# A Mamba stage on one core: two sequences as one run of 18 rounds, the output product moved within the round, its squares summed first, and the projection blocks spread anew

## The chip, the cores and the metric

The kernel runs on one core of one Trainium2 chip. The metric is the device time of one execution of the whole program in microseconds (us): everything from the first load to the last store. Engines are named as in the profile: PE is TensorE (PEld its weight loads), DVE is VectorE, ACT is ScalarE, POOL is GpSimd, SP issues the DMAs.

## What is computed

The program is a small model of two layers: a Mamba-2 block, a gated MLP, a second gated MLP with weights from a 16-entry table, an attention of 16 heads, and a mixture of 8 experts. The change touches the Mamba block alone. It works on 2 sequences (batches) of 1024 tokens, 256 wide, in float32:

```
zxbcdt = x @ in_proj_w
z, xb, Bc, Cc, dt = split(zxbcdt)                  # 512, 128, 128, 512, 8 columns
xBC = silu(causal_depthwise_conv([xb, Bc, Cc]))    # 4 taps, 768 channels
dt = softplus(dt + dt_bias);  A = -exp(A_log)
# for each chunk of 128 tokens and each of 8 heads (head size 64, state size 64):
#   Y_diag = (C B^T * exp(seg), masked) @ (x dt)      inside the chunk
#   Y_off  = exp(cum) * C @ state                     from the chunks before
#   state  = decay * state + B^T @ (decayed x dt)     goes to the next chunk
y = Y_diag + Y_off + D * x
y = rmsnorm(y * silu(z)) @ out_proj_w
```

The state begins at zero for each of the two sequences, and the convolution sees zeros before the first token of each.

## The kernel before

**Tiling.** Tokens come in 16 tiles (chunks) of 128, 8 for each sequence, and in 4 groups of 512. A float32 product is made of three passes of split operands (high by high, high by low, low by high; `three_passes`, L53 to L55). For each group of 512 tokens the input projection gives ten blocks of 128 channels: six that go through the convolution (m = 0 to 5, "conv") and four of the gate z (m = 6 to 9, "z"). One conv block is six matmuls on PE, two evacuations on ACT (L1048, L1051), three taps and a small copy on DVE (L1127, L1132 or L1134), a tanh on ACT (L1100), and a last product on DVE that writes `xbc` (L1194, `conv_end`), one block later. One z block is six matmuls, a tanh on ACT (L1059) and one product on DVE (L1142).

**The chunk.** A chunk n is worked in three events, in three successive rounds. Event A, on PE: two transposes (L965), the broadcast of the cumulated decay `rows` (L972, which waits for `steps` of POOL, made anew each four chunks, L1245), the scores C B^T (L980, which wait until `mixed` of the chunk before is done, since they overwrite its bank), and the mask (L986, which waits for `row_exp`); on ACT the copy `xb_tok` (L1064), `row_exp` (L1069) and the eight exponentials `decay` (L1075). `A_end`, on DVE: `mixed` = decay times scores, eight instructions (L1149). Event B: the products y (L999 and L1005) and the new state's product (L1014) on PE; the state's update and `gated` (L1156 to L1170) on DVE; `gated_hi` and `squares` on ACT (L1082, L1083); `gated_lo` on POOL (L1267). Event C: the output product (12 matmuls, L53 to L55 with `out_hi`, `out_lo`) and behind it the sum of the squares (4 products with a vector of ones, 8 instructions in the trace, L1026), both into one bank; DVE makes `out_var` (L1174), POOL `out_root` (L1263), and in `C_end` DVE scales and adds (`u_tok`, L1178).

**What sets the order.** Each engine has its own instruction stream, written out by `sequence_steps` in one list that all engines follow; waits are semaphores. Round c holds, in this order: A(c); then the projection blocks of place 0; B(c-1) and C(c-2); place 1 (empty); A_end(c) and C_end(c-2); the blocks of place 2. `SPREAD` puts the ten blocks of the next group into four rounds: conv 0, 1 | conv 2, 3 | conv 4 ahead of B, conv 5 and z 6 behind | z 7 ahead of B, z 8 and 9 behind. The rounds run from 0 to 9 for each sequence: two more than there are chunks, so that B and C of the last ones are done. A loop of one turn (`Fori`) does the first sequence, and the code is written out once more for the second. All ten blocks of the very first group come ahead of the first round.

**Banks.** Projection blocks and C share two PSUM banks in turn (`with_banks`): a block waits until the user before last of its bank is finished with on ACT or DVE. B has bank 5, the scores have 2 and 3, rows and mask 0 and 1.

**Around it.** In the second sequence, rounds 5 and 6 also hold the splitting of MLP weights (`feed`: ACT L1088, POOL L1219 to L1228), and rounds 7 to 9 the norm of the first MLP group (stats L155 to L165, apply L202, turn L224, split L238). SP loads those weights when all projections and convolutions are done, and the inputs of the table stage when the whole Mamba stage is done.

Of the kernel before, what the change touches and what calls it, by code (L numbers as in the profile page):

```python
# [14 lines left out]
P = 128  # L15
# [684 lines left out]
def mamba_stage(nc, sems, mem, s, w, dma, u, ff, norm_next):  # L700
# [11 lines left out]
    def sb(what, shape, dt=F32):  # L712
# [5 lines left out]
             "xdt_decayed skip_ready y_ready y_taken state_ready state_done gated gated_hi squares gated_lo out_ready out_var "  # L718
# [32 lines left out]
    SPREAD = ((2, 2), (2, 2), (0, 2, 2), (0, 2, 2))  # L751

    QUARTERS = 4
    FEED_AT = {5: (0, 1), 6: (2, 3)}
    NORM_AT = {7: ("stats",), 8: ("apply", "turn"), 9: ("split",)}
    NORM_BANK = 2

    def sequence_steps(last):


        steps = []
        for c in range(CHUNKS + 2):
            group = c // TG + 1
            blocks = []
            if group <= (1 if last else GB):
                first = sum(len(x) for x in SPREAD[:c % TG])
                blocks = [(place, ("project", group, first + n)) for n, place in enumerate(SPREAD[c % TG])]
            parts = [[("A", c, None)] if c < CHUNKS else [],
                     ([("B", c - 1, None)] if 1 <= c <= CHUNKS else []) + ([("C", c - 2, None)] if c >= 2 else []),
                     ([("A_end", c, None)] if c < CHUNKS else []) + ([("C_end", c - 2, None)] if c >= 2 else [])]  # L770
            for place, part in enumerate(parts):
                steps += part + [e for at, e in blocks if at == place]
            if last:
                steps += [("feed", c, n) for n in FEED_AT.get(c, ())] + [("norm", c, n) for n in NORM_AT.get(c, ())]
        return steps

    first_steps = [("project", 0, m) for m in range(IP)]
    PER = dict(conv=GB * XBC_BLOCKS, z=GB * Z_BLOCKS, chunk=CHUNKS)
# [5 lines left out]
    def with_banks(events):  # L784


        ring = [e for e in events if e[0] in ("project", "C")]
        assert len(ring) % 2 == 0
        at = {e: n for n, e in enumerate(ring)}
        users = [("C", e[1], None) if e[0] == "C_end" else e for e in events]  # L790
        return [(e, s.psum[:, 6 + at[user] % 2, :], ring[at[user] - 2] if at[user] >= 2 else None) if user in at
                else (e, None, None) for e, user in zip(events, users)]

    def sequences(engine, step, start=None):

        for e in with_banks(first_steps):
            step(0, *e)
# [5 lines left out]
        if start:  # L803
            start(BATCH - 1)
        for e in with_banks(sequence_steps(True)):
            step(BATCH - 1, *e)

# [118 lines left out]
    def tensor(pe):  # L926
# [10 lines left out]
        def step(b, e, bank, old):  # L937
            kind, c, m = e
            n = CHUNKS * b + (c or 0)
            par = (c or 0) // TG % 2  # L940
            q = slice((c or 0) % TG * P, (c or 0) % TG * P + P)
            if kind in ("project", "C"):

                if old is None and c != 0:

                    pe.wait_ge(done["out_done"], CHUNKS * b)
                    pe.wait_ge(done["gate_done"], PER["z"] * b + Z_BLOCKS)
                elif old is not None and old[0] == "C":
                    pe.wait_ge(done["out_done"], CHUNKS * b + old[1] + 1)
                elif old is not None:  # L950
# [1908 lines left out]
```

## Time and profile before

| | us |
|---|---|
| median of 3 runs (lowest, highest) | 1872.57 (1870.99, 1872.8) |
| the profiled execution | 1873.78 |
| its span in the profile | 1872.0 |
| from the first projection block to the end of `mixed` of chunk 1 | 58.38 to 111.52 |
| from there to the end of `mixed` of the last chunk | 111.52 to 332.32 |
| from there to the first product of the MLP | 332.32 to about 349.7 |

The profile is one execution. Its page gives the busy time of each engine over the span; the stage of this case takes 58 to 350 us of 1872. A good mark for the rounds is the end of `mixed` (the eight DVE instructions of L1149): it comes once in each round, and the time from one to the next is called an interval here.

### The profile page before, as it was taken

The numbers are of one execution on the slowest core, as the hardware profiler recorded it, in microseconds if no ns is written. First come the engines' busy times: TensorE is split into PE (matmuls) and PEld (weight loads), VectorE is DVE, ScalarE is ACT, GpSimd is POOL, SyncE is SP. The second block draws the span as 40 slices with busy tenths as digits, with TensorE's granted clock in tenths as the row PEclk, the third lists the DMA queues.
The fourth block names the chain that finished last, engine by engine and source line by source line (L and its number), as shares of the span: only waits on it lengthen the run. The fifth ranks groups of instructions, "written<-read, shape, count | busy, mean of one in ns | idle before, by whom it ended". The sixth has DMA issues, their size and how long they took to land.

```text
span 1872.0 us, 31589 instructions
## 1 busy us (share of the span) xinstructions
PE 1623.4 (87%) x9546; PEld 1356.6 (72%) x9546; DVE 1246.1 (67%) x2797; ACT 972.2 (52%) x2046; POOL 656.7 (35%) x727
## 2 busy tenths in 40 slices
PE   3578778788899999999999997999999999858795
PEld 2345444677788878888888886788888888746584
DVE  6677474678965666666666675766666666758585
ACT  3355354355533375666666754656666666424242
POOL 5133336433433342223222312322233222355652
PEclk9789788899999999999999998999999999879897
DMA  3000001200010420000000000010000000231243
GB/s 108 1 1 1 1 1 46 63 12 14 5 21 1 107 70 17 8 22 22 22 0 22 6 18 23 1 46 2 22 22 22 0 22 6 84 125 57 95 135 128
DMA packets 78383, 64.53 MB, mean 34 GB/s; under 512 B 16656, under 2 KB 72704, under 8 KB 78288
## 3 DMA queue, kind: packets, MB, share of 16 engines
q1 hardware_dynamic: 74544, 53.08, 10.0%
q0 software_dynamic: 3744, 10.26, 1.5%
q8 instruction: 50, 0.82, 0.2%
q14 instruction: 45, 0.37, 0.1%
HBM read 44.89 MB, written 18.43 MB: 34 GB/s over the span
## 4 chain that ended last, share of the span: by engine, by line
PE 64%; DVE 17%; issue 6%; ACT 5%; DVEq 3%; POOL 3%; DMA 1%; POOLq 0%; ACTq 0%; SPq 0%
PE psum L53 10%; PE psum L55 10%; PE psum L54 10%; PE psum L1687 6%; PE psum L1700 3%; PE psum L1677 3%; PE psum L1679 3%; PE psum L1678 3%; PE psum L1701 3%; PE psum L1708 3%; DVE table_leaves L589 2%; DVE mamba_conv_sum L1127 2%; POOL moe_slots_x L2173 2%; DVE mamba_mixed L1149 2%; PE psum L999 1%
## 5 line engine op out<-in xcount | busy, mean ns | idle before, releaser
L1888 POOL TENSOR_SCALAR attn_probs<-attn_probs,attn_inverse 128x128 f32<-128x128 f32 (+7 forms) x256 | 192.3, 751 | 543.6 <-DVE attn_inverse L1839 543.6
L1756 ACT ACTIVATE attn_pt_hi<-psum 128x512 fp32r<-128x512 f32 (+3 forms) x384 | 185.4, 484 | 182.7 <-PE psum L1687 181.9
L1761 ACT ACTIVATE attn_probs<-attn_probs,attn_neg_max 128x128 f32<-128x128 f32 (+7 forms) x256 | 198.4, 775 | 134.0 <-DVE attn_neg_max L1811 131.5
L1807 DVE TENSOR_TENSOR attn_pt_lo<-psum,attn_pt_hi 128x512 fp32r<-128x512 f32 (+3 forms) x384 | 211.8, 553 | 43.1 <-ACT attn_pt_hi L1756 39.4
L1687 PE MATMUL psum<-ident,attn_probs 128*128 128x128 f32 x1152 | 194.0, 278 | 15.5 <-DVE x_tok L1847 11.9
L1811 DVE CUSTOM_DVE_ANT_0 attn_probs<-psum,attn_mask 128x128 f32<-128x128 f32 (+7 forms) x256 | 192.7, 753 | 20.1 <-PE psum L1679 10.6
L1700 PE MATMUL psum<-attn_pt_hi,attn_v_hi 128*128 128x512 f32 (+3 forms) x384 | 161.2, 420 | 21.7 <-DVE attn_pt_lo L1807 12.4
L1687 PEld LDWEIGHTS psum<-ident,attn_probs 128*128 128x128 f32 x1152 | 140.3, 142 | 40.3 <-issue 12.9
L417 POOL TENSOR_TENSOR gated_h_lo<-gated_hidden,gated_h_hi 128x512 fp32r<-128x512 f32 x56 | 79.6, 1421 | 161.0 <-ACT gated_h_hi L402 161.0
L1677 PE MATMUL psum<-attn_k_hi,attn_q_hi 128*128 128x512 f32 (+3 forms) x384 | 133.6, 348 | 2.6 <-DVE attn_neg_max L1811 2.4
L1701 PE MATMUL psum<-attn_pt_lo,attn_v_hi 128*128 128x512 f32 (+3 forms) x384 | 134.4, 350 | 0.0
L1679 PE MATMUL psum<-attn_k_hi,attn_q_lo 128*128 128x512 f32 (+3 forms) x384 | 133.5, 348 | 0.0
L1678 PE MATMUL psum<-attn_k_lo,attn_q_hi 128*128 128x512 f32 (+3 forms) x384 | 133.4, 347 | 0.0
L1708 PE MATMUL psum<-attn_pt_hi,attn_v_lo 128*128 128x512 f32 (+3 forms) x320 | 116.0, 362 | 0.0
L1881 POOL TENSOR_TENSOR attn_qkv_lo<-attn_qkv_raw,attn_qkv_hi 128x512 fp32r<-128x512 f32 x45 | 57.9, 1289 | 153.6 <-ACT attn_qkv_hi L1738 153.6
L53 PE MATMUL psum<-act_hi,attn_qkv_hi 128*128 128x512 f32 x256 | 105.5, 412 | 4.4 <-POOL attn_qkv_lo L1881 2.2
L55 PE MATMUL psum<-act_hi,attn_qkv_lo 128*128 128x512 f32 x256 | 102.5, 400 | 0.0
L54 PE MATMUL psum<-act_lo,attn_qkv_hi 128*128 128x512 f32 x256 | 102.3, 400 | 0.0
L1700 PEld LDWEIGHTS psum<-attn_pt_hi,attn_v_hi 128*128 128x128 f32 x384 | 74.1, 193 | 31.5 <-DVE attn_pt_lo L1807 16.8
L402 ACT ACTIVATE gated_h_hi<-gated_hidden 128x512 fp32r<-128x512 f32 x56 | 35.3, 630 | 108.6 <-DVE gated_hidden L462 108.6
L1804 DVE SCALAR_TENSOR_TENSOR attn_q_lo<-psum,attn_bias,attn_q_hi 128x512 fp32r<-128x512 f32 x64 | 48.1, 751 | 60.8 <-ACT attn_q_hi L1754 59.8
L1804 DVE SCALAR_TENSOR_TENSOR attn_k_lo<-psum,attn_bias,attn_k_hi 128x512 fp32r<-128x512 f32 x64 | 48.0, 749 | 60.2 <-ACT attn_k_hi L1754 60.2
(382 smaller groups left out, 4875.2 us busy)
## 6 DMA issues: line engine op xcount, KB each, us to landing
moe_xrow<-moe_slots_x SPq DMA_DIRECT2D x46, 129.0 KB, 2.1
moe_slots_x<-attn_z_raw SPq DMA_DIRECT2D x4, 1032.0 KB, 12.2
attn_qkv_raw<-in_L_attn_W_Q_dram SPq DMA_DIRECT2D x32, 128.0 KB, 2.3
attn_qkv_raw<-in_L_attn_W_K_dram SPq DMA_DIRECT2D x32, 128.0 KB, 2.5
attn_qkv_raw<-in_L_attn_W_V_dram SPq DMA_DIRECT2D x32, 128.0 KB, 2.6
attn_wo_raw<-in_L_attn_W_O_dram SPq DMA_DIRECT2D x16, 256.0 KB, 3.1
moe_weights_raw<-_L_ffn_gate_up_proj_dram SPq DMA_DIRECT2D x8, 512.0 KB, 6.0
x_in<-_attn_hidden_states_dram SPq DMA_DIRECT2D x4, 512.0 KB, 5.6
```

Source lines behind the costliest of these rows:

```text
L53: pe.matmul(out, s_hi, m_hi, start=start, stop=False)
L54: pe.matmul(out, s_hi, m_lo, start=False, stop=False)
L55: return pe.matmul(out, s_lo, m_hi, start=False, stop=stop)
L1677: pe.matmul(view[:, at:end], q_hi, k_hi, start=True, stop=False)
L1679: last = pe.matmul(view[:, at:end], q_lo, k_hi, start=False, stop=True)
L1687: last = pe.transpose(s.psum[:, work_bank(e), lq * P:(lq + 1) * P], probs_block(e, TG * e["g"] + lq), s.ident[:, :])
L1700: pe.matmul(s.psum[:, 7, at:], v_hi, p_hi[:, at:], start=j == 0, stop=False, skip_group_check=True)
L1701: pe.matmul(s.psum[:, 7, at:], v_hi, p_lo[:, at:], start=False, stop=False, skip_group_check=True)
L1761: act.activation(probs_view(e), probs_view(e), ACT.Exp, bias=stat(neg_max, e), scale=-1.0, accum_out=stat(sums, e)).then_inc(exp_done, 1)
L1807: dve.tensor_tensor(lo, work_view(e), hi.bitcast(F32), ALU.subtract).then_inc(work_done, 1)
L1811: dve.tensor_tensor_reduce(probs_view(e), score_view(e), mask[:, (QT - 1 - e["t"]) * P:], -SCORE_SCALE, -MASKED, ALU.add, ALU.min, stat(ne ...
L1888: pool.tensor_scalar(probs_view(e), probs_view(e), stat(inverse, e), 1.0, ALU.mult, ALU.mult).then_inc(probs_ready, 1)
```

## The change

The two sequences become one list of 18 rounds for 16 chunks; no loop is left, and the state is set to zero behind chunk 7 in the place of its update. An event that was A is now three: `rows` (transposes, rows, scores), `decay` (mask and exponentials), `mix`. A round n is now: `rows`(n); `out`(n-2) with `out_end`(n-2) (formerly C and C_end); the blocks of place 0; `decay`(n); `y`(n-1) (formerly B); `mix`(n); the blocks of place 1. In `out` the squares come ahead of the product, into one column of bank 5, and have a semaphore step of their own; y(n) waits until `out_var`(n-1) has read that column. `out_end` waits for root and product. The blocks of the next group stand at: conv 0, 1 behind mix | z 6 ahead of decay, conv 2 and z 7 behind | conv 3 ahead, conv 4 and z 8 behind | conv 5 ahead, z 9 behind. The four z blocks of the very first group move into round 0. On POOL the root comes first in a round.

```diff
-    SPREAD = ((2, 2), (2, 2), (0, 2, 2), (0, 2, 2))
+    LATER = (((), (0, 1)), ((6,), (2, 7)), ((3,), (4, 8)), ((5,), (9,)))
+    OPENING = (6, 7), (8, 9)
...
+    def blocks_of(n, place):
+
+        group, at = n // TG + 1, n % TG
+        later = LATER[at][place] if group < GROUPS else ()
+        opening = OPENING[place] if n == 0 else ()
+        return [("project", 0, m) for m in opening] + [("project", group, m) for m in later]
+
+    def sequence():
+
+        steps = [("project", 0, m) for m in range(XBC_BLOCKS)]
+        for n in range(TILES + 2):
+            if n < TILES:
+                steps.append(("rows", n, None))
+            if n >= 2:
+                steps += [("out", n - 2, None), ("out_end", n - 2, None)]
+            steps += blocks_of(n, 0)
+            if n < TILES:
+                steps.append(("decay", n, None))
+            if 1 <= n <= TILES:
+                steps.append(("y", n - 1, None))
+            if n < TILES:
+                steps.append(("mix", n, None))
+            steps += blocks_of(n, 1)
...
-        with engine.Fori(0, BATCH - 1) as b:
-            if start:
-                start(b)
-            for e in with_banks(sequence_steps(False)):
-                step(b, *e)
...
                 pe.wait_ge(done["y_taken"], n)
+                pe.wait_ge(done["out_var"], n)
...
-            elif kind == "C":
+            elif kind == "out":
+                pe.wait_ge(done["squares"], n + 1)
+                for m in range(Z_BLOCKS):
+                    last = pe.matmul(s.psum[:, 5, 0:1], squares[:, m, :], s.ones[:, 0:1], start=m == 0,
+                                     stop=m == Z_BLOCKS - 1)
+                last.then_inc(done["out_sums"], 1)
+
                 pe.wait_ge(done["gated_lo"], n + 1)
...
-                if c < CHUNKS - 1:
+                if n % CHUNKS == CHUNKS - 1:
+                    dve.memset(state[:, :, :], 0.0).then_inc(done["state_done"], 1)
+                else:
...
+            elif kind == "out_end":
                 dve.wait_ge(done["out_root"], n + 1)
+                dve.wait_ge(done["out_sums"], 2 * n + 2)
```

## Rows read from the trace of the kernel before

**Rows 1.** The page, part 1: busy time of each engine over the span.

```profile
PE 1623.4 (87%) x9546; PEld 1356.6 (72%) x9546; DVE 1246.1 (67%) x2797; ACT 972.2 (52%) x2046; POOL 656.7 (35%) x727
```

**Rows 2.** Busy time by stretch: length, engines' busy time (instructions), granted clock, DMA.

```profile
58.38:96.74 38.36, 26.27 (x86) 17.64 (x86) 23.39 (x43) 20.22 (x38) 5.06 (x5) 0.86 0.00 0
96.74:111.52 14.78, 10.57 (x46) 5.34 (x46) 10.65 (x21) 6.55 (x18) 4.70 (x6) 0.77 0.00 1
111.52:130.49 18.97, 11.27 (x62) 7.08 (x62) 15.24 (x28) 10.18 (x24) 6.21 (x7) 0.82 0.00 0
...
146.24:158.86 12.62, 10.73 (x66) 6.65 (x66) 6.56 (x16) 6.40 (x16) 5.35 (x7) 1.00 0.00 1
...
210.36:234.94 24.58, 19.29 (x96) 13.50 (x96) 6.95 (x18) 7.21 (x17) 8.00 (x9) 0.79 0.00 1
...
267.57:285.43 17.86, 16.19 (x72) 9.94 (x72) 10.24 (x22) 7.37 (x18) 7.18 (x8) 0.73 0.00 0
...
298.04:308.72 10.68, 9.06 (x54) 4.75 (x54) 5.17 (x14) 4.66 (x15) 5.25 (x7) 0.82 0.00 0
...
332.32:349.64 17.32, 11.36 (x72) 9.03 (x72) 9.43 (x25) 2.52 (x4) 8.47 (x14) 0.80 0.03 5
```

**Rows 3.** Instructions by line and shape, 60 to 340 us: busy, mean ns.

```profile
L1149 DVE SCALAR_TENSOR_TENSOR mamba_mixed<-mamba_decay,mamba_step_dt,psum 128x128 f32<-128x128 f32 x128 | 34.5, 342 | 13.4 <-ACT mamba_decay L1075 11.1 <-issue 2.3
...
L1194 DVE SCALAR_TENSOR_TENSOR mamba_xbc<-mamba_conv_th,mamba_conv_sum 128x512 f32<-128x512 f32 x24 | 19.3, 804 | 0.5
```

**Rows 4.** Instructions in order of time, the opening: start, duration, engine.

```profile
61.32 0.60 ACT L1048 ACTIVATE mamba_conv_in<-psum 128x512 f32<-128x512 f32 x1 [3.98 <-PE psum L55]
...
62.68 2.40 DVE L1127 SCALAR_TENSOR_TENSOR mamba_conv_sum<-mamba_conv_in,conv_w,mamba_conv_sum 128x512 f32<-128x512 f32 x3 [4.53 <-ACT mamba_conv_sum L1051]
...
83.96 0.79 PE L53 MATMUL psum<-act_hi,in_hi 128*128 128x512 f32 x1 [5.50 <-DVE mamba_zs L1142]
```

**Rows 5.** The same, two rounds with conv blocks.

```profile
174.71 0.50 PE L53 MATMUL psum<-act_hi,in_hi 128*128 128x512 f32 x1 [1.64 <-DVE u_tok L1178]
...
178.25 3.27 DVE L1127 SCALAR_TENSOR_TENSOR mamba_conv_sum<-mamba_conv_in,conv_w,mamba_conv_sum 128x512 f32<-128x512 f32 x3 [0.16 <-issue]
178.34 1.19 ACT L1069 ACTIVATE mamba_row_exp<-psum 64x512 f32<-64x512 f32 x2
...
187.66 0.42 DVE L1156 TENSOR_TENSOR mamba_state<-mamba_state,mamba_row_exp 128x256 f32<-128x256 f32 x1
...
189.26 0.69 DVE L1170 TENSOR_TENSOR mamba_gated<-mamba_gated,mamba_zs 128x512 f32<-128x512 f32 x1
```

**Rows 6.** The same, between the two sequences.

```profile
219.86 0.55 PE L53 MATMUL psum<-out_hi,mamba_gated_hi 128*128 128x256 f32 x1 [2.22 <-POOL mamba_gated_lo L1267]
...
222.56 1.02 PE L1026 MATMUL psum<-ones,mamba_squares 128*128 128x1 f32 x8
...
224.37 1.90 POOL L1245 TENSOR_TENSOR mamba_steps<-mamba_cum_rows,mamba_own_row 128x1024 fp32r<-128x1024 f32 x1
...
232.77 2.15 DVE L1149 SCALAR_TENSOR_TENSOR mamba_mixed<-mamba_decay,mamba_step_dt,psum 128x128 f32<-128x128 f32 x8 [7.57 <-ACT mamba_decay L1075]
```

**Rows 7.** The same: scores and y at either level, stats, scaling of an output.

```profile
104.41 1.97 PE L1005 MATMUL psum<-mamba_c_scaled,mamba_state 64*64 64x128 f32 x16
...
235.26 1.13 PE L980 MATMUL psum<-mamba_xbc 64*128 64x512 f32 x4
...
298.07 2.08 PE L980 MATMUL psum<-mamba_xbc 64*128 64x512 f32 x4 [1.64 <-DVE mamba_mixed L1149]
...
336.50 0.17 DVE L165 TENSOR_SCALAR norm_mlp_var<-norm_mlp_var 128x4 f32<-128x4 f32 x1
...
339.70 0.48 DVE L1178 SCALAR_TENSOR_TENSOR u_tok<-psum,mamba_out_root,u_tok 128x256 f32<-128x256 f32 x1 [0.66 <-POOL mamba_out_root L1263]
```

**Rows 8.** The chain that ended last, in order of time, a round without blocks.

```profile
303.78 0.32 PE psum L53
...
305.41 0.80 PE psum L1026 x8
```

More of the change, by code:

```diff
@@ L750, in mamba_stage @@
     GB = SEQ // GROUP
-    SPREAD = ((2, 2), (2, 2), (0, 2, 2), (0, 2, 2))
+    LATER = (((), (0, 1)), ((6,), (2, 7)), ((3,), (4, 8)), ((5,), (9,)))
+    OPENING = (6, 7), (8, 9)
     QUARTERS = 4
-    FEED_AT = {5: (0, 1), 6: (2, 3)}
-    NORM_AT = {7: ("stats",), 8: ("apply", "turn"), 9: ("split",)}
+    FEED_AT = {CHUNKS + 5: (0, 1), CHUNKS + 6: (2, 3)}
+    NORM_AT = {CHUNKS + 7: ("stats",), CHUNKS + 8: ("apply", "turn"), CHUNKS + 9: ("split",)}
     NORM_BANK = 2
[L758 to L774, printed above, removed]
-        return steps
@@ L777, in mamba_stage @@
-    first_steps = [("project", 0, m) for m in range(IP)]
-    PER = dict(conv=GB * XBC_BLOCKS, z=GB * Z_BLOCKS, chunk=CHUNKS)
+    def blocks_of(n, place):
[18 more added lines that the diff above has]
+            steps += blocks_of(n, 1)
+            steps += [("feed", n, m) for m in FEED_AT.get(n, ())] + [("norm", n, m) for m in NORM_AT.get(n, ())]
+        return steps
@@ L794, in sequences @@
[L794 to L806 removed]
+    events = with_banks(sequence())
+    projects = [e for e, _, _ in events if e[0] == "project"]
@@ L935, in tensor @@
         pe.wait_ge(done["masks"], 4)
[L937 to L950, printed above, removed]
-                    what, at = place_of(old)
-                    pe.wait_ge(done["evacuated"] if what == "conv" else done["gate_done"], PER[what] * b + at + 1)
+        for (kind, n, m), bank, old in events:
+            group, par = n // TG, n // TG % 2
+            q = slice(n % TG * P, n % TG * P + P)
+            if old is not None and old[0] == "out":
+                pe.wait_ge(done["out_done"], old[1] + 1)
+            elif old is not None:
+                what, at = place_of(old)
+                pe.wait_ge(done["evacuated"] if what == "conv" else done["gate_done"], at + 1)
             if kind == "project":
@@ L1106, in vector @@
         dve.drain()
[L1108 to L1117 removed]
+        dve.memset(state[:, :, :], 0.0).then_inc(done["state_done"], 1)
+        for e, bank, _ in events:
+            kind, n, m = e
+            par, q = n // TG % 2, slice(n % TG * P, n % TG * P + P)
             dve.drain()
@@ L1122, in step @@
                 if what == "conv":
-                    dve.wait_ge(done["evacuated"], PER["conv"] * b + at + 1)
+                    dve.wait_ge(done["evacuated"], at + 1)
                     acc = conv_sum[:, at % 3, :]
```

193 lines of the change are left out of this document (86 added, 107 removed).

## The prediction

> **What bounds the kernel now.** I read the page first: PE is busy 87% of the span and DVE 67% [rows 1], but the change lies in 58 to 350 us, so the share of the whole says little. Next come the stretches, cut at each end of `mixed` [rows 2]. In an interval with three conv blocks DVE works 15.2 of 19.0 us; in one without blocks it works 5.2 of 10.7 and PE 9.1, at a granted clock of 0.82. So no engine is full everywhere. Where conv blocks stand, DVE's queue sets the pace; where none stand, it is a chain that goes from engine to engine. The instructions in order of time show how. In a round with blocks the second block behind `mixed` starts only when `u_tok` has freed its bank, 1.64 us late, and `row_exp` stands on ACT behind a conv tanh that waits for DVE's taps [rows 5]; mask and y wait for `row_exp`. In a round without blocks the chain of waits is: `mixed`, scores, mask, y, state, output product, squares, `out_var`, `mixed`; a piece of it is [rows 8]. Between the sequences one interval takes 24.6 us [rows 2], twice its neighbours: B and C of the last chunks run alone, the output product waits 2.2 us for `gated_lo`, `steps` are only made at 224.37, and `mixed` waits 7.6 us for the exponentials [rows 6].
>
> **Prices.** The taps of a conv block take 2.40 us [rows 4]; with the small copy and the gaps 2.8, with `conv_end` (a 128x512 instruction; 0.69 undisturbed, mean 0.80 [rows 3]) 3.4 to 3.5. The same taps took 3.27 just as `row_exp` released POOL's work [rows 5], so I put 0.4 to 0.8 of stretch on each interval with conv blocks. `mixed` takes 34.5 us for 16 chunks [rows 3], so 2.16, with its gaps 2.3. DVE's part of y takes from 187.66 to 189.95, 2.3 [rows 5]; I use 2.35. A z block costs DVE 0.75 (a 128x512 instruction like L1170, 0.69 [rows 5]). The root makes DVE wait 0.66, and `u_tok` takes 0.48, with gaps 0.55 [rows 7]. The evacuation of a conv block takes 61.32 to 62.68, 1.35 [rows 4]. On PE the price depends on the granted level: scores 1.1 at 2.4 GHz and 2.1 at 1.2 GHz [rows 7]; mask half of that; y (L999 and L1005, alike) 2.0 and 3.9 from L1005's slow 1.97 [rows 7]; output product 1.63 [rows 8] and, from 219.86 to 222.56, 2.7 [rows 6]; squares 0.8 and 1.0 [rows 6, 8]; a block (half as many matmuls, twice the columns) like the output product, 1.5 and 2.6.
>
> **The change, interval by interval.** Time zero is the end of mix(n); each interval ends with mix(n+1).
>
> *Without blocks ahead of it* (3 to 4, 7 to 8, 11 to 12 with one z block that fits in, and 12 to 15). PE: scores 1.1, squares to 1.9, product to 3.5, mask to 4.05, y to 6.1. `decay` on ACT is done at about 6.3 and hides. DVE's y ends at 8.5, mix at 10.8. The serial chain is thus: scores, squares, product, mask, y, DVE's y, mix. The one of before is: scores, mask, y, state 0.6, product, squares, `out_var` 0.3, mix, 9.4 at the high level. So this part is a loss of 1.4: DVE's y, which used to run beside the output product, is now in series. All at the low level it is 15.3. PE now sits idle for 2 to 4 us while DVE does y and mix. Before, after a gap of 1.64 the scores took 2.08, the low level [rows 7]; I therefore price scores, squares and half of the product low: 12.5.
>
> *Two conv and a z block* (4 to 5, 8 to 9). Both conv blocks are now projected while DVE does y and mix, since their banks are free. DVE: 2.8, 3.4, `out_var` 0.3, root 0.66, `u_tok` 0.55, z 0.75, y 2.35, mix 2.3: 13.1, with the stretch 13.9. y on PE must wait for `out_var` at 6.5 (bank 5), ends at 8.5 and hides. Before: 14.8 in the like interval [rows 2].
>
> *Conv 2, z 7 | conv 3* (three times). DVE: 3.4, 0.75, `out_var`, root and `u_tok` to 5.7. Conv 3 gets its bank when z 7 is done (4.2), is projected by 5.7 to 6.8 and evacuated by 7.1 to 8.2, so DVE waits 1.4 to 2.5. Taps and `conv_end` 3.4, y 2.35, mix 2.3: 15.2 to 16.3, with the stretch 16.2. *Conv 4, z 8 | conv 5* (three times) adds a second `conv_end`, 0.75, and starts behind a PE gap: 17.2. Before, these places took 19.0 and up to 17.9 [rows 2].
>
> Sum from the end of mix(1) to that of mix(15): 2 x 13.9 + 3 x 16.2 + 3 x 17.2 + 3 x 12.5 + 2 x 12.5 + 13.5 = 204.0. The last (14 to 15) has 1.0 more, because `out_root` now stands behind the weight splitting on POOL and DVE's y behind it. The stretch of before is 332.32 - 111.52 = 220.8: **16.8 less**, of which some 12 is the interval between the sequences (24.6 becomes 12.5) and some 5 the rest. As a test of the method, the interval of 12.62 us at full clock [rows 2] comes out by the same steps, z 9 behind `u_tok` and the chain of before, at 12.3.
>
> *Opening.* Conv blocks 0 to 5 run as before. z 6 and z 7, which ran on PE beside DVE's taps, now come behind the scores of chunk 0 and ahead of its mask; before, z 8 and z 9 stood ahead of all of these, after a PE gap of 5.5 us [rows 4]. Two blocks in place of two: mix(0) ends about where it did. Then z 8 and z 9 must leave their banks before conv 0 and 1 can start, behind mix(0): DVE idles about 2 us. I add **2.0**; from 0 (z in time) to 5 (all low).
>
> *Tail.* From 332.32 to 349.64, 17.3 us. The stats end on DVE 4.3 us into it [rows 7], and `out_var`(14), hence y(15), now waits behind them; then DVE's y, apply, turn, squares, product, split: 15.8 to 18.7 by the two levels. Before, product and squares stood ahead of `out_var`; now the product covers the root. I take **-0.3**.
>
> *The rest.* Waits, drains and instruction counts stay. POOL's reordering inside a round is hidden: it has 5.4 us of work in 10 or more. SP's loads of `up` and `down` follow the last block; both it and their users come earlier by like amounts. After the stage nothing has a date of its own, so its gain should arrive in full: I put 0 there, and 3 us to either side for TensorE's clock, whose levels may fall elsewhere.
>
> Net: -16.8 + 2.0 - 0.3 = -15.1. The profiled execution of 1873.8 becomes 1858.7. The median of before, 1872.57, is 1.2 lower, so it becomes **1857.5**.
>
> **A rule against the change.** PE worked at the low level for at least 2.08 us behind a gap of 1.64 [rows 7], and 267.57 to 285.43 ran at 0.73 [rows 2]. The Trainium skill, "TensorE: Matmul & The Clock Gate", section "HAM oscillation", says that waits between bursts of matmuls bring the clock down again each time. By that rule the sum would go towards the low ends. The trace agrees in part: one interval of before stayed at 1.00 [rows 2].
>
> **Rivals.**
> (a) *The clock holds.* PE's work is denser in conv rounds and the low level rare: intervals 10.8, 13.4, 15.4, 16.2, sum about 188, no loss in the opening: -34 us, 1839. For it: the interval at 1.00. Against: the new PE gaps. Middle of this case 1846. Chance 0.17.
> (b) *The serial order costs more.* PE is low through most of the rounds without blocks and conv 3 and 5 arrive late: 13.3 in place of 12.5 for each of six, 0.6 more for each of six others: -15 + 5 + 4 = -6, between -2 and -9, about 1866. Chance 0.22.
> (c) *Slower.* PE falls to the low level behind every gap and stays there: 6 x 15.3 + 1, 2 x 15.5, 18.3 and 19 three times, 236 against 220.8; with opening and tail +18, 1890. Since all high is 188 plus about 3 for POOL and stretch, the balance tips where some six tenths of the rounds run low: a mean granted clock of about 0.69. The lowest interval here had 0.73 [rows 2], so this is unlikely. Chance 0.06.
> (d) *The gain is swallowed,* by a load that becomes late or by the boundary's cost staying as `steps` and `xb_tok` waits: the 24.6 stays near 22 and the rest brings 1 to 4. Against it: without the loop `steps` has a whole round of slack. Chance 0.07.
>
> **How the numbers follow.** The forecast (-10 to -22) has 0.48. The range: (a)'s middle end and most of (b): 1842 to 1868, leaving out the far end of (a), a slice of (b), and (c) and (d). A measurement of this kernel can tell about 0.2%, 3.7 us, from no change. Faster: 0.48 + 0.17 + most of (b) 0.18 + a bit of (d) 0.02 = 0.85. Same: 0.04 + 0.04 = 0.08. Slower: (c) and 0.01 of (d) = 0.07.
>
> **What would show it.** In the stretches from mix to mix: 24.6 gone to 11 to 14; intervals with conv 2 to 5 at 15 to 18 with DVE over 80% busy; those without blocks not below 10.7, perhaps longer than before; the granted clock above 0.75. The wait of PE for `u_tok` should be gone, and DVE's wait for L1005 should have grown. It would be wrong if mix(1) ended later than 116, if rounds 12 to 15 took over 14 each, or if the stretch behind 350 us changed its length by more than 3.

## The result, and the profile of the changed kernel

The changed kernel takes **1880.61 us** (median of 6 runs, 1878.31 to 1881.21), the kernel before 1872.58 (6 runs on the same chip, 1869.52 to 1872.8). The ratio is 1.0047, with a 95% interval of 1.0036 to 1.0058: **8.0 us slower**. Forecast were 1857.5, in a range of 1842 to 1868. The time lies outside the range and the sign is wrong.

The page, part 1, of after, which answers to [rows 1]. The instructions are the same but for one; PE is busy 9 us longer with them (1623.4 before) and DVE 3 us less:

```profile
PE 1632.3 (87%) x9546; PEld 1367.1 (73%) x9546; DVE 1242.9 (66%) x2798; ACT 970.3 (52%) x2046; POOL 653.9 (35%) x727
```

Busy time by stretch, after (length, then PE, PEld, DVE, ACT, POOL with their instructions, granted clock, DMA). Each stretch runs from one end of `mixed` to the next, but for the last line, which runs from the end of the last `mixed` to the first product of the MLP. They answer to [rows 2]:

```profile
96.68:114.25 17.57, 15.11 (x68) 9.30 (x68) 12.46 (x25) 9.50 (x22) 4.74 (x6) 0.90 0.00 1
114.25:129.97 15.72, 12.18 (x72) 7.84 (x72) 11.92 (x26) 8.55 (x22) 6.16 (x7) 1.00 0.00 0
148.12:162.58 14.46, 13.91 (x66) 9.02 (x66) 5.85 (x15) 5.08 (x15) 5.36 (x7) 0.75 0.00 1
162.58:176.71 14.13, 12.18 (x72) 7.81 (x72) 11.69 (x25) 8.19 (x21) 5.29 (x7) 1.00 0.00 1
...
259.67:278.69 19.02, 14.24 (x66) 9.04 (x66) 13.45 (x26) 9.12 (x23) 7.17 (x8) 0.72 0.26 89
294.33:308.60 14.27, 10.92 (x54) 6.65 (x54) 5.17 (x15) 4.67 (x14) 5.32 (x7) 0.76 0.00 0
308.60:322.93 14.33, 10.97 (x54) 6.55 (x54) 5.17 (x15) 5.70 (x16) 8.91 (x11) 0.75 0.01 2
338.58:357.27 18.69, 12.35 (x69) 10.28 (x68) 9.57 (x26) 2.52 (x4) 7.98 (x13) 0.68 0.01 2
```

Read the clock column: some rounds ran at 1.00, others at 0.72 to 0.76. All 15 intervals from mix(0) on, in us: before 14.8, 19.0, 15.8, 12.6, 15.2, 18.5, 17.8, **24.6**, 14.0, 18.6, 17.8, 12.6, 10.7, 12.1, 11.5; after 17.6, 15.7, 18.1, 14.5, 14.1, 17.7, 20.2, **14.4**, 14.2, 16.5, 19.0, 15.6, 14.3, 14.3, 15.7. The eighth, between the sequences, gave back 10.2 us, those with conv 2, z 7 and conv 3 3.3, 0.8 and 2.1, the fifth 1.1. All others lost: 2.8 in the opening, 1.9 and 3.0 in the other two rounds with one z block, 2.3, 2.4 and 1.2 in those with conv 4 and 5, 0.2 in the ninth, 3.6, 2.2 and 4.2 in the last three. mix(0) ends at 96.7 in both. The sum from mix(1) to mix(15) is 338.6 - 114.3 = 224.3 us (before 220.8, forecast 204.0). The last step of the stage (`split`) starts at 355.93 in place of 348.22; what follows takes 1523.6 us in place of 1523.8. So the whole loss (7.5 us between the two profiled spans) comes from the stage: +2.8 opening, +3.5 rounds, +1.4 tail. The rounds as one stretch, after:

```profile
114.25:338.58 224.33, 180.78 (x907) 113.64 (x907) 132.65 (x288) 99.50 (x245) 91.73 (x98) 0.80 0.03 10
```

PE spends 180.8 us on 907 matmuls at a clock of 0.80. In the kernel before it spent 170.4 on 908 at 0.85, from 111.52 to 332.32. DVE's work fell from 135.6 to 132.7. The same products (a record or two can be missing from a trace) have become 10 us dearer.

Where an interval without blocks goes is seen in its chain. Instructions in order of time, after, the interval that ends with the `mixed` of chunk 14 (rows of PE and DVE; in brackets the idle time before, and who ended it):

```profile
308.66 1.82 PE L964 MATMUL psum<-mamba_xbc 64*128 64x512 f32 x4 [2.83 <-DVE mamba_mixed L1124]
...
310.41 1.86 PE L1007 MATMUL psum<-ones,mamba_squares 128*128 128x1 f32 x8
...
312.13 0.56 PE L53 MATMUL psum<-out_hi,mamba_gated_hi 128*128 128x256 f32 x1
...
314.85 1.08 PE L971 MATMUL psum<-mamba_mask,mamba_ident_b 128*128 128x512 bf16 x2
...
315.85 1.08 PE L985 MATMUL psum<-mamba_mixed,mamba_xb_tok 128*64 128x512 f32 x4
...
319.69 0.93 DVE L1147 TENSOR_TENSOR mamba_gated<-mamba_gated,mamba_zs 128x512 f32<-128x512 f32 x1
320.78 2.15 DVE L1124 SCALAR_TENSOR_TENSOR mamba_mixed<-mamba_decay,mamba_step_dt,psum 128x128 f32<-128x128 f32 x8 [0.16 <-issue]
```

PE has nothing to do for 2.83 us (1.64 before [rows 7]). Then scores (L964), squares (L1007), product (L53 to L55, from 312.27 to 315.04 in the chain) and mask (L971) all run at the 1.2 GHz level; the first y product, 1.08 for four in the instructions (1.98 at the low level), is the first at 2.4 GHz. The chain of waits, in order of time, gives each one's share without overlap (start, length, what):

```profile
308.66 1.82 PE psum L964 x4
310.48 1.79 PE psum L1007 x8
...
315.04 0.88 PE psum L971 x2
315.92 1.01 PE psum L985 x4
316.93 1.02 PE psum L991 x16
317.95 0.61 PE psum L1000 x4
```

Added up: 1.82 + 1.79 + 2.77 + 0.88 + 2.03 (y) + 0.61 (state), then 4.4 of DVE: 14.3.

So it is behind every long wait of the changed kernel. From mix(1) on, PE waits for `mixed` ahead of the scores for over 2.3 us nine times (2.39 to 3.41), and each of the nine intervals has a granted clock of 0.61 to 0.76. In the other five the wait is 0.75 us or less, the scores and squares behind it are at 2.4 GHz (1.13 and 1.05), and the clock of the interval is 0.86 to 1.00. Six of the nine scores are low themselves (1.82 or 2.08). In the other three (130.01, 259.72, 294.39) the level falls just behind them, as here:

```profile
294.39 1.21 PE L964 MATMUL psum<-mamba_xbc 64*128 64x512 f32 x4 [2.83 <-DVE mamba_mixed L1124]
295.52 1.86 PE L1007 MATMUL psum<-ones,mamba_squares 128*128 128x1 f32 x8
```

### The profile page after: what moved, and what is told of

Its sections match the earlier page's. It is cut to its first block, busy times and chain, and to the rows that moved or that the text cites. A ratio compares the mean times of both kernels' runs of the same rounds, so it can differ in the third digit from the quotient of the medians.

```text
span 1879.5 us, 31630 instructions
## 1 busy us (share of the span) xinstructions
PE 1632.3 (87%) x9546; PEld 1367.1 (73%) x9546; DVE 1242.9 (66%) x2798; ACT 970.3 (52%) x2046; POOL 653.9 (35%) x727
## 4 chain that ended last, share of the span: by engine, by line
PE 63%; DVE 19%; issue 6%; ACT 4%; DVEq 4%; POOL 3%; DMA 1%; POOLq 0%; SPq 0%; ACTq 0%
PE psum L53 10%; PE psum L55 9%; PE psum L54 9%; PE psum L1657 6%; PE psum L1670 3%; PE psum L1647 3%; PE psum L1649 3%; PE psum L1648 3%; PE psum L1671 3%; PE psum L1678 3%; DVE table_leaves L589 2%; DVE mamba_conv_sum L1102 2%; POOL moe_slots_x L2143 2%; DVE mamba_mixed L1124 2%; DVE gated_hidden L462 1%
## 5 line engine op out<-in xcount | busy, mean ns | idle before, releaser
L1657 PE MATMUL psum<-ident,attn_probs 128*128 128x128 f32 x1152 | 192.8, 277 | 15.5 <-DVE x_tok L1817 11.9
L1670 PE MATMUL psum<-attn_pt_hi,attn_v_hi 128*128 128x512 f32 (+3 forms) x384 | 161.2, 420 | 23.7 <-DVE attn_pt_lo L1777 14.5
L53 PE MATMUL psum<-act_hi,attn_qkv_hi 128*128 128x512 f32 x256 | 105.3, 411 | 4.4 <-POOL attn_qkv_lo L1851 2.2
L55 PE MATMUL psum<-act_hi,attn_qkv_lo 128*128 128x512 f32 x256 | 101.9, 398 | 0.0
L1670 PEld LDWEIGHTS psum<-attn_pt_hi,attn_v_hi 128*128 128x128 f32 x384 | 74.0, 193 | 33.3 <-DVE attn_pt_lo L1777 18.7
```

What stands on the lines that cost most here:

```text
L53: pe.matmul(out, s_hi, m_hi, start=start, stop=False)
L55: return pe.matmul(out, s_lo, m_hi, start=False, stop=stop)
L1657: last = pe.transpose(s.psum[:, work_bank(e), lq * P:(lq + 1) * P], probs_block(e, TG * e["g"] + lq), s.ident[:, :])
L1670: pe.matmul(s.psum[:, 7, at:], v_hi, p_hi[:, at:], start=j == 0, stop=False, skip_group_check=True)
```

## The experiments

They ran in three batches, each beside the kernel before; its medians were 1872.58, 1871.04 and 1870.56 us (19, 16, 17 runs). I compare ratios across batches. Diffs show the edit to the changed kernel, unless said otherwise.

**1. The single list alone.** The new 18 rounds with the order, the squares' place, the spread and the opening of before.

```diff
-    LATER = (((), (0, 1)), ((6,), (2, 7)), ((3,), (4, 8)), ((5,), (9,)))
-    OPENING = (6, 7), (8, 9)
+    LATER = (((), (0, 1)), ((), (2, 3)), ((4,), (5, 6)), ((7,), (8, 9)))
+    OPENING = (), ()
...
-        steps = [("project", 0, m) for m in range(XBC_BLOCKS)]
+        steps = [("project", 0, m) for m in range(IP)]
```

The rest of its edit is that of run 2.

> Changed kernel with everything but the single list of rounds undone: the order in a round, the place of the squares, the spread of the blocks, the opening and the root's place on POOL are those of before. Theory S (the new order inside a round costs what the missing gap between the sequences gains): the interval between the sequences falls from 24.6 to about 12.5, all others stay, 1860 us, ratio to before 0.9935. Rival B (the new spread and opening of the blocks cost it): the same, 1860. Rival N (the gap between the sequences was no loss, because its work comes later anyway): 1870 to 1874.

Measured: 1863.8 us (1860.58 to 1865.06), ratio 0.995 [0.9937, 0.9964]. Busy time by stretch, the interval at the boundary:

```profile
209.22:221.92 12.70, 10.73 (x66) 6.64 (x66) 5.69 (x15) 6.42 (x16) 5.87 (x7) 1.00 0.01 1
```

The interval of 24.6 us [rows 2] is 12.7, as long as its like at 146 us. The single list is thus worth some 12 us at its place and 9 as a whole. The other edits together must have lost 17 to 18.

**2. The order undone.** Blocks spread and opened as in the change, but the order of before, with the squares behind the product and in its bank, and the root late on POOL.

```diff
-            if n >= 2:
-                steps += [("out", n - 2, None), ("out_end", n - 2, None)]
-            steps += blocks_of(n, 0)
...
+            steps += blocks_of(n, 0)
...
+            if n >= 2:
+                steps.append(("out", n - 2, None))
...
+            if n >= 2:
+                steps.append(("out_end", n - 2, None))
...
-                pe.wait_ge(done["out_var"], n)
...
+                    last = pe.matmul(bank[:, D:D + 1], squares[:, m, :], s.ones[:, 0:1], start=m == 0,
```

> Changed kernel, with the order in a round of before (rows, mask and decay, blocks, y, product and squares, mix, scaling), squares behind the product in the product's bank, root late on POOL; the single list, the new spread and the new opening stay. Theory S: the intervals without blocks go back from 14.3 to 11 to 12.5 and the whole to 1855 to 1864. Rival B: it stays at 1872 or above, since the spread and the opening are still the new ones.

Measured: 1867.12 (1861.39 to 1869.68), 0.9971 [0.996, 0.9982]. The last intervals return to 11.6, 10.9, 10.7 and 12.1. Under the old order the new spread and opening cost 3.3 us beside run 1; the new order costs 14 on top of that.

**3. The mask first.** Mask and exponentials directly behind the scores, all else as in the change.

```diff
+            if n < TILES:
+                steps.append(("decay", n, None))
             if n >= 2:
                 steps += [("out", n - 2, None), ("out_end", n - 2, None)]
             steps += blocks_of(n, 0)
-            if n < TILES:
-                steps.append(("decay", n, None))
```

> Changed kernel, but mask and decay stand right behind the scores, ahead of squares and output product. Theory S says that the length of the chain scores, squares, product, mask, y, DVE's y, mix counts, not the place of the mask in it: intervals without blocks stay at 14 to 14.5, the whole at 1880 plus or minus 3. Rival M (the exponentials come too late, because the mask now stands behind the output product and a block): 1870 or less, above all in the rounds with conv 3 and conv 5, whose exponentials now wait on ACT behind the evacuation.

Measured: 1899.71 (1899.21 to 1901.89), 1.0148 [1.0134, 1.0162], far above the 1880 expected. The intervals without blocks are 14.2, 14.2 and 13.3: the place of the mask matters little there, the sum of the series counts. But those with conv blocks are 18 to 21. In order of time, PE, this kernel:

```profile
174.66 1.03 PE L971 MATMUL psum<-mamba_mask,mamba_ident_b 128*128 128x512 bf16 x2 [4.03 <-ACT mamba_row_exp L1051]
175.49 1.71 PE L1007 MATMUL psum<-ones,mamba_squares 128*128 128x1 f32 x8
```

The mask waits 4.03 us for `row_exp`, which stands on ACT behind a conv tanh (172.63) that waits for DVE's taps, and now squares, product and z block are queued behind that wait. This is what the new order is good for: with the product between, the mask of the same chunk in the changed kernel (167.81) has no wait before it. The sum of the prediction had the mask hidden there, which was right, but put no number on what that saves.

**4. The squares last.** Order of the change, but the eight one-column products stand behind the output product, still in bank 5.

```diff
             elif kind == "out":
+                pe.wait_ge(done["gated_lo"], n + 1)
+                for m in range(Z_BLOCKS):
+                    last = three_passes(pe, bank[:, 0:D], pair_at((gated_hi, gated_lo), slice(None), m),
...
                 pe.wait_ge(done["squares"], n + 1)
...
-                pe.wait_ge(done["gated_lo"], n + 1)
```

> Changed kernel, but the squares are summed behind the output product, still in bank 5 and still ahead of mask and y. Theory S: the same work stands in the same series, only out_var and root come later, so the scaling u_tok is late by 0.8 to 1 more in rounds without blocks, hidden by y on PE: 1880 to 1884. Rival Q (the squares ahead of the product are what costs, 1.8 us at 1.2 GHz): 1872 to 1876.

Measured: 1873.46 (1870.35 to 1875.59), 1.0003 [0.9994, 1.0012], 7 us less than the changed kernel, where no gain was expected; the rival, 1872 to 1876, is what came. The last intervals are 12.6, 13.5, 13.6. In order of time, PE, the same interval (`mixed` of chunk 14) in this kernel:

```profile
303.77 2.08 PE L964 MATMUL psum<-mamba_xbc 64*128 64x512 f32 x4 [2.83 <-DVE mamba_mixed L1125]
...
308.50 1.27 PE L1013 MATMUL psum<-ones,mamba_squares 128*128 128x1 f32 x8
309.63 0.59 PE L971 MATMUL psum<-mamba_mask,mamba_ident_b 128*128 128x512 bf16 x2
```

The gap is the same 2.83, and the scores are low too. But the mask is at the high level (0.59 for two; 1.08 in after), and the squares take 1.27, not 1.86. The squares start low and end high: 4.7 us after the start of the scores PE is still at the low level here (303.77 to 308.50), in the changed kernel it is for 7.2 (308.66 to the first y at 315.85). Why the level returns sooner with the squares last isn't shown.

**5. The gap filled.** 20 more matmuls (128x256) behind the rows and ahead of the scores, in rounds 3 to 15 except 6 and 10, into the bank that the output product of the round overwrites next. Nothing is left out; PE's work grows.

```diff
+                if n >= 3 and (n > 12 or n % 4 != 2):
+                    fill_bank, fill_old = out_at[n - 2]
...
+                    for k in range(20):
+                        pe.matmul(fill_bank[:, 0:D], w["out"][0][:, 0, 0:P], w["out"][0][:, 1, :], start=True, stop=True)
```

> Changed kernel with 20 more matmuls (128x256, the output weights with themselves, into the bank of the coming output product, overwritten there) on PE behind the rows broadcast, where PE waits 2.8 us for mix; in rounds 3 to 15 except those behind an interval with two conv blocks in a row (6 and 10). Nothing is left out. Theory C (most of the loss is PE at 1.2 GHz behind that gap): the matmuls take 2.2 us at 2.4 GHz, the clock stays high, the intervals without blocks fall from 14.3 to 11 to 12, the whole to 1858 to 1868. Rival L (the loss is the length of the chain at any clock, or the clock does not answer to this work): intervals stay at 14 or grow by the 1 to 2 us by which slow fill overruns the gap, 1880 to 1900.

Measured: **1862.9** (1862.27 to 1863.86), 0.9955 [0.9941, 0.9968]: 17 us less than the changed kernel, by useless work. Busy time by stretch (the rounds as one, and the interval to chunk 14) and instructions in order of time, PE:

```profile
114.47:323.84 209.37, 180.61 (x1127) 123.84 (x1128) 132.97 (x288) 99.45 (x245) 92.14 (x98) 0.95 0.03 11
299.30:310.52 11.22, 10.38 (x74) 6.97 (x74) 5.25 (x15) 5.77 (x16) 9.00 (x11) 1.00 0.01 2
```

```profile
296.48 2.66 PE L970 MATMUL psum<-out_hi 128*128 128x256 f32 x20
299.39 1.13 PE L974 MATMUL psum<-mamba_xbc 64*128 64x512 f32 x4 [0.24 <-DVE mamba_mixed L1134]
300.45 1.05 PE L1017 MATMUL psum<-ones,mamba_squares 128*128 128x1 f32 x8
...
302.87 0.60 PE L981 MATMUL psum<-mamba_mask,mamba_ident_b 128*128 128x512 bf16 x2
```

The same series of work takes 11.2 in place of 14.3, with scores, squares and mask at the high level. 1127 matmuls, 220 more, now keep PE busy as long as the 907 did (180.8 us), at a clock of 0.95. In the chain of waits of this kernel (start, length, what):

```profile
299.39 1.13 PE psum L974 x4
300.52 0.98 PE psum L1017 x8
...
303.03 0.45 PE psum L981 x2
```

Beside the chain of the changed kernel, the scores are 0.7 us shorter, the squares 0.8, the product 1.2 (1.53 in place of 2.77), the mask 0.4; y, the state's product and DVE's part are as long as there. That is the whole 3.1, and this is the direct test of the cause: nothing but PE's idleness ahead of the scores was altered. It did not pay everywhere. In the rounds with conv 4, z 8 and conv 5 (19.4, 20.3 and 21.1 in place of 18.1, 20.2 and 19.0) the bank comes free late, the filling runs at the low level itself and ends behind `mixed`. In order of time, PE, this kernel:

```profile
256.02 4.64 PE L970 MATMUL psum<-out_hi 128*128 128x256 f32 x20 [2.62 <-ACT mamba_conv_sum L1043]
```

The stage is 14.8 us shorter (`split` starts at 341.15). The other 2.8 of the two profiled runs lie behind it, where nothing was changed; why isn't shown.

**6. The spread undone.** New order, with the blocks and the opening of before.

```diff
-    LATER = (((), (0, 1)), ((6,), (2, 7)), ((3,), (4, 8)), ((5,), (9,)))
-    OPENING = (6, 7), (8, 9)
+    LATER = (((), (0, 1)), ((), (2, 3)), ((4,), (5, 6)), ((7,), (8, 9)))
+    OPENING = (), ()
```

> Changed kernel with the order in a round kept, but the spread of the projection blocks and the opening of before (all ten blocks of the first group ahead; conv 0, 1 | conv 2, 3 | conv 4 ahead of mask, conv 5 and z 6 behind mix | z 7 ahead, z 8 and 9 behind). Theory S (the order costs it): intervals without blocks stay at 14.3, conv ones sum as before or worse, 1878 to 1890. Rival B (the new spread costs it): 1860 to 1870.

Measured: 1866.39 (1862.83 to 1867.82), 0.9972 [0.996, 0.9984]: 14 us less than the changed kernel. With the old spread two blocks (z 8 and 9) stand between the `mixed` of a group's last round and the next scores in PE's order, and one (z 9) with the new, so PE has work during more of its wait. In order of time, PE, the scores of chunk 12 in the changed kernel and in this one, in that order:

```profile
278.74 2.08 PE L964 MATMUL psum<-mamba_xbc 64*128 64x512 f32 x4 [3.09 <-DVE mamba_mixed L1124]
```

```profile
268.62 1.13 PE L964 MATMUL psum<-mamba_xbc 64*128 64x512 f32 x4 [0.62 <-DVE mamba_mixed L1124]
```

Between 120 and 340 us the scores wait over 2.3 us nine times in the changed kernel and six times here. The changed kernel's intervals of 14.5, 14.4 and 15.6 are 12.7, 10.2 and 12.7 here.

**7. The squares in the gap.** Squares between rows and scores, where PE waits anyway; mask behind the scores, product behind y.

```diff
-                steps += [("out", n - 2, None), ("out_end", n - 2, None)]
+                steps.append(("sums", n - 2, None))
...
+                steps += [("scores", n, None), ("decay", n, None)]
...
+            if n >= 2:
+                steps.append(("out", n - 2, None))
```

> Changed kernel with the squares summed between the rows broadcast and the scores, where PE waits for mix anyway (they need nothing of this round), mask and decay right behind the scores, the output product behind y (beside DVE's y), the scaling u_tok behind mix; single list, new spread and new opening. Theory S: the chain of a round is scores, mask, y, DVE's y, mix, 8.3 us with PE high and about 11 low; intervals without blocks 9 to 11.5, the whole 1845 to 1860. Rival G (each such shift only opens another gap in which the clock falls, and the conv rounds wait for row_exp again as in the run with the mask first): 1865 or more.

Measured: 1868.59 (1867.25 to 1870.95), 0.9988 [0.9979, 0.9997]; 1845 to 1860 was expected. The part without blocks came near the forecast of 9 to 11.5: 10.3, 10.9 and 11.9. The three rounds with conv 4, z 8 and conv 5 took 20.6, 23.4 and 23.3, where the changed kernel has 18.1, 20.2 and 19.0. In order of time, PE, this kernel:

```profile
263.05 0.79 PE L53 MATMUL psum<-act_hi,in_hi 128*128 128x512 f32 x1 [5.86 <-DVE u_tok L1161]
```

With the product behind y its bank comes free only after mix, so the blocks wait 5.86 us for `u_tok`: the wait that the change had removed (1.64 [rows 5]) is back, and larger.

The squares in the gap did not keep the level up. PE waits only 0.82 to 1.62 us ahead of them in rounds 12 to 15, yet the scores behind them are low in all four (2.08). In order of time, PE, this kernel:

```profile
294.88 1.05 PE L1012 MATMUL psum<-ones,mamba_squares 128*128 128x1 f32 x8 [0.83 <-ACT mamba_squares L1071]
296.06 2.08 PE L969 MATMUL psum<-mamba_xbc 64*128 64x512 f32 x4
```

**8. The same with the old spread and opening.** The edit of run 6 on top of run 7.

```diff
-    LATER = (((), (0, 1)), ((6,), (2, 7)), ((3,), (4, 8)), ((5,), (9,)))
+    LATER = (((), (0, 1)), ((), (2, 3)), ((4,), (5, 6)), ((7,), (8, 9)))
```

> The kernel with the squares in the gap (order as there), with the spread of the blocks and the opening of before. If the new spread and opening are worth something by themselves (the prediction put 5 us on it), this is 3 to 8 us above the run with the squares in the gap and the new spread; if they cost, as the two runs with the old order hint at (1867.1 against 1863.8), it is 2 to 6 us below.

Measured: 1884.76 (1879.96 to 1885.37), 1.0061 [1.0047, 1.0075]: 16 us above run 7, where 3 to 8 above or 2 to 6 below were expected. The intervals behind mix(3), mix(7) and mix(11), which have z 8 and z 9 here, are 17.6, 12.0 and 17.6, and a block waits 5.09 us for `u_tok` at 272.24. So the old spread, 14 us better than the new one in the order of the change (run 6), is 16 us worse in this order.

**9. The opening undone.** Only the four z blocks of the first group stand ahead of the first round again.

```diff
-    OPENING = (6, 7), (8, 9)
+    OPENING = (), ()
...
-        steps = [("project", 0, m) for m in range(XBC_BLOCKS)]
+        steps = [("project", 0, m) for m in range(IP)]
```

> Changed kernel, but all ten blocks of the first group stand ahead of round 0 again; the spread of the later groups stays new. The end of mix(1) was 111.5 before, 114.3 in the changed kernel and 111.7 with spread and opening both undone. If the opening is worth those 2.7 us and nothing else, the whole is 1877 to 1879 and the spread of the later groups holds the other 11 of the 14 us by which undoing both helped. Rival: much of the 14 is the opening (clock and phase of all that follows), 1870 or less.

Measured: 1874.36 (1870.76 to 1879.89, 12 runs), 1.0021 [1.0011, 1.0031], some 5 to 6 us less than the changed kernel and between the two expectations. Busy time by stretch, chunk 0 to chunk 1:

```profile
96.50:110.50 14.00, 11.37 (x52) 6.28 (x52) 11.34 (x23) 7.14 (x19) 4.70 (x6) 0.88 0.00 1
```

17.57 is 14.00 again: 3.6 us at the place itself. The runs of this kernel lie 9 us apart and the profiled one (1879.09) near its highest, with its rounds 2.2 us longer than those of the changed kernel (226.5), so where the other 2 are isn't shown.

**10. Gap filled, old spread.** Run 6 with the 20 matmuls in rounds 3, 7, 11, 13, 14 and 15, those whose scores in run 6 stood behind a gap of 2.6 us or more.

```diff
+                if n >= 13 or n % 4 == 3:
...
+                    for k in range(20):
```

> New order with the spread and opening of before (1866.4 without fill), plus the 20 filling matmuls in rounds 3, 7, 11, 13, 14, 15, where PE waited 2.6 to 2.8 us for mix. Theory C (clock behind the gap): the three intervals without blocks fall from 15.7, 14.3 and 14.3 to 11, those behind the other three gaps by 1 to 2 each: 1850 to 1858. Rival: spread and fill repair the same loss, so that little is left to gain: 1862 to 1866.

Measured: **1854.74** (1852.94 to 1857.37), 0.9914 [0.9901, 0.9927]. 11 us less than run 6; the last four intervals are 11.2, 11.2, 11.2 and 13.4. This is the lowest median of all, 0.86% (16 us) below before for the same output.

**11. Gap filled, old order.** Run 1 with 12 such matmuls in rounds 13 to 15.

```diff
+                if n >= 13:
...
+                    for k in range(12):
```

> The run with the single list alone (order, squares and blocks of before, 1863.8) plus 12 filling matmuls in rounds 13 to 15, where PE waited 1.6 to 2.1 us for mix. Theory C: those three intervals (12.2, 10.8, 11.5) fall to 9.5 to 10, the whole to 1858 to 1861; and the order of before is then 1.2 to 1.6 us a round shorter than the new one (11.1 filled), the bare price of the order. Rival: no change, 1863 to 1866.

Measured: 1858.11 (1853.32 to 1859.12), 0.9922 [0.991, 0.9935]. Busy time by stretch, the intervals to chunks 13 and 14:

```profile
287.71:297.00 9.29, 9.26 (x67) 5.96 (x66) 5.19 (x15) 4.71 (x15) 5.32 (x7) 1.00 0.01 2
297.00:306.28 9.28, 9.28 (x67) 5.96 (x66) 5.43 (x14) 5.67 (x17) 8.85 (x10) 1.00 0.00 1
```

At full clock the old series is 9.3, the new one 11.2: that is the price of the order alone, 1.9 us for each such round (forecast 10.8 against 9.4). It also shows that the gap was costly under the old order as well: the last three intervals are 12.2, 10.8 and 11.5 without the fill (run 1), and 9.3, 9.3 and 10.7 with it. The 5.2 us by which these three are shorter are the 5 us of the whole.

**12. Two orders.** Order of the change to round 12, that of run 7 from 13 on, old spread, fill of 20 in rounds 3, 7 and 11 and of 6 from 13 on.

```diff
+            early = n >= 13
...
+            if n >= 2 and early:
+                steps.append(("sums", n - 2, None))
...
+                    for k in range(6 if n >= 13 else 20):
```

> Attempt at a version that beats both: single list, spread and opening of before, new order up to round 12, and from round 13 on the order with the squares in the gap and the output product behind y; 20 filling matmuls in rounds 3, 7, 11, 6 in rounds 13 to 15. Theory: the last three intervals fall to 8.5 to 10 (10.3 in the run with the squares in the gap, at a clock of 0.83), the whole to 1846 to 1853. Rival: the order change in the middle costs a wait of its own, or six matmuls are too few to keep the clock: 1855 or more.

Measured: 1855.04 (1850.11 to 1858.67), 0.9914 [0.99, 0.9929], 2 us above the top of the expected 1846 to 1853 and at the rival's 1855. The last four intervals are 11.2, 10.3, 9.4 and 10.8, 4 us less than in run 10 (the last `mixed` ends at 310.2 in place of 314.2), but the medians don't differ. 2.5 of these 4 are lost in the tail (the `split` starts at 330.12, in run 10 at 331.57), the rest behind it: 1521.4 us there, 1523.3 here, in one profile each. Whether the latter is more than chance is open; run 5 has 1520.8.

## Why the prediction was wrong

The series of work was foreseen, and so was PE's idle time ahead of the scores. What failed is the price of PE's work behind that idle time: it was put between the two levels, and it ran at the low one.

**The sum by itself.** With runs 1, 2 and 6 the 8 us split in two ways: -9.4 (list, ratio 0.995) + 4.1 (order, from 0.995 to 0.9972) + 14.0 (spread and opening, from there to 1.0047) = 8.8, near the measured ratio; or -9.4 + 3.9 (spread and opening) + 14.2 (order). Order and spread cost about 4 each alone, and 18 together. The prediction had a gain of 12 for the list, and one of 5 for "the rest".

**Bounds, prices, boundary: right.** DVE's prices held (`mixed` 2.15, taps 2.40). 24.6 became 12.7 with the list alone; the step that put it at 12.5 was right in its mechanism. In the whole change it was 14.4, at a clock of 0.69.

**Intervals without blocks: the series right, the clock wrong.** Serial order costing 1.4 was right in kind (1.9 by run 11), and at full clock the 10.8 came as 11.2 (run 5). The step that failed is "I therefore price scores, squares and half of the product low: 12.5". It took the squares at 1.0 from a row that was no low one [rows 6]: at full clock the same eight instructions show 1.05 in run 5. The 0.8 beside it [rows 8] is from the chain, which counts no overlap, and not a second level. And it let the clock return within the product. Measured in the chain were squares 1.79, the whole product 2.77 and the mask 0.88, all low, where 1.0, 2.2 and 0.55 had been put. That is 0.8 + 0.6 + 0.3 = 1.7 of the 1.8 by which 12.5 became 14.3; the scores took 0.3 less than put (1.82), and the state's product and DVE's part 0.3 more. The gap itself, 2 to 4 us, stood in the text; the bound of 15.3 was there as well, and the value should have been nearer to it. For the three last intervals the sum had 12.5, 12.5, 13.5; they measured 14.3, 14.3, 15.7. In the last, `u_tok` waits 3.51 us for the root behind the weight splitting, for which 1.0 was put. But it is done at 331.04, and the chain runs over PE until 334.27, so this wait cost nothing. The 1.4 by which 15.7 exceeds 14.3 is the low level again, which there lasts through scores (2.08) and y (3.16 in place of 2.03). In order of time, PE, after:

```profile
330.44 1.98 PE L985 MATMUL psum<-mamba_mixed,mamba_xb_tok 128*64 128x512 f32 x4
```

**Rounds with a single z block.** Priced at 12.5 too, they took 14.5, 14.4 and 15.6 (7.0 more in three). That the z block "fits in" was right, but z 9 stands behind mix(3), mix(7) and mix(11) alone, so PE idled 2.39, 3.41 and 3.09 us before the scores, and then, in the first of them, was busy 13.9 of 14.5 us at a clock of 0.75. This is the place where the spread matters: with two blocks there (run 6) the same intervals took 12.7, 10.2 and 12.7, so the sign of "some 5 the rest" was wrong. Run 8 shows that this holds for the order of the change and not for any order.

**Conv 4, z 8 | conv 5.** 17.2 forecast, 18.1, 20.2 and 19.0 measured. In order of time, DVE, after:

```profile
265.21 0.48 DVE L1156 SCALAR_TENSOR_TENSOR u_tok<-psum,mamba_out_root,u_tok 128x256 f32<-128x256 f32 x1 [0.66 <-POOL mamba_out_root L1221]
269.06 2.40 DVE L1102 SCALAR_TENSOR_TENSOR mamba_conv_sum<-mamba_conv_in,conv_w,mamba_conv_sum 128x512 f32<-128x512 f32 x3 [3.36 <-ACT mamba_conv_sum L1033]
```

Squares, product and conv 5 are in series on PE at the low level (260.78 to 267.44), so DVE waits 3.36 us where 1.4 to 2.5 was put. That the level is the cause here is argued from these rows; the filling of run 5 came too late in these rounds to test it. *Conv 2, z 7 | conv 3*, at a clock of 0.86 to 1.00, was 15.7, 17.7 and 16.5 for a forecast of 16.2; *two conv and a z* 14.1 and 14.2 for 13.9. So the method holds where the clock does. Of the 20.3 us between 204.0 and 224.3, the three rounds with one z block make 7.0, the last three 5.8, those with conv 4 and 5 5.7, and all others 1.8.

**Opening and tail.** 2.0 was put on the opening, 2.8 measured. DVE, after, the first taps behind mix(0):

```profile
101.89 2.41 DVE L1102 SCALAR_TENSOR_TENSOR mamba_conv_sum<-mamba_conv_in,conv_w,mamba_conv_sum 128x512 f32<-128x512 f32 x3 [3.61 <-ACT mamba_conv_sum L1033]
```

They wait 3.61, not 2, because conv 0 stands behind a wait of PE for `zs` and runs at the low level (97.55 to 100.49, 2.9 us). In order of time, PE, after:

```profile
97.55 0.79 PE L53 MATMUL psum<-act_hi,in_hi 128*128 128x512 f32 x1 [2.50 <-DVE mamba_zs L1117]
```

 The tail was put at -0.3 and measured +1.4, within the 15.8 to 18.7 of its working: `u_tok` waits 1.40 us for the root, and the last squares (1.71 at 350.77) are at the low level. Its clock is 0.68 (0.80 before [rows 2]).

**The rivals.** Rival (c) is what happened, in two thirds: 224.3 lies between the forecast's 204.0 and its 236, and the level falls behind each of the nine long gaps, at the scores or just behind them, but does not stay low to the end of the interval. It had a chance of 0.06. Its balance was to tip "where some six tenths of the rounds run low", and nine of the fifteen intervals had a clock of 0.61 to 0.76, among them all six without conv blocks. That was right. The step that failed is the next one, "a mean granted clock of about 0.69": the mean was 0.80, because a round that runs low is at 0.7 and not at 0.5. Held against 0.69, and against a lowest interval of 0.73 [rows 2], (c) looked unlikely; held against the number of gaps, which the forecast itself made longer, it was not. Rival (b) had the right mechanism with 0.8 us for each of six intervals, where it was 1.8 to 3.1. Of the announced signs of error, "if rounds 12 to 15 took over 14 each" was the one that came; mix(1) ended at 114.3 (under 116) and the part behind 350 us kept its length.

On the rule quoted against the change: behind gaps of 2.39 to 3.41 us six of nine scores took 1.8 to 2.1 us, the low level, the other three were followed by it, and closing most of the gaps gave 17 us back. The Trainium skill, "TensorE: Matmul & The Clock Gate", section "HAM oscillation", describes this pattern for a kernel whose bursts of matmuls wait for DMAs. The trace agrees in all nine, for waits between engines; the prediction weighed the rule in words, and put too little of it into the sum.

## What to carry over

When a change puts work in series behind a wait of PE, price all of PE's work that follows the wait at 1.2 GHz until a row of a like gap shows where the level returned, and give the case in which it does not return the chance that the row gives it. Look which blocks stand in an engine's gaps before they are spread anew. And of edits made together, price the pair: here each cost 4 us alone and 18 together, and the spread that was better by 14 us in one order was worse by 16 in another.

## What was not expected of the hardware

Useless work paid: 20 matmuls of 128x256 (2.66 us) ahead of the scores made the interval behind them 3.1 us shorter (14.33 to 11.22), and 12 of them (1.70 us) did the same for the old order (12.2 and 10.8 became 9.3). Eight products with a single column take 1.79 us at the low level, more than half of a product of twelve 128x256 matmuls at 2.77, and their place behind it saved 7 us on the whole (run 4). Put into the gap, they did not keep the level up (run 7), and wide matmuls did (run 5). What brings the level back, and why it falls at the scores behind one gap of 2.6 us and only behind them at another, isn't shown by these runs.
